# Short attentions with their scores in two halves and other products between; third one with three groups combined ahead and blocks 1, 2, 2, 3, 3

## What is computed

```
h = tok(x)                                   # patches @ W + b + positions
h = LN(h + attn0(h))   # 12 heads of 16, scores minus 0.2 x 3x3 neighbour sum, softmax
h = LN(h + ffn0(h))    # causal attention, then 8 experts, top 2, capacity
h = LN(h + attn1(h))   # scale per head, diagonal masked, projection with bias
h = LN(h + ffn1(h))    # 4 layers: attention (12 heads of 64, relative bias), FFN, experts in 2 of them
```

## Time and profile before

| | us |
|---|---|
| three runs | 1920.93, 1916.85, 1915.08 |
| median | 1916.85 |
| the profiled execution, its own time | 1923.19 |
| its span in the profile | 1921.4 |
| mean granted TensorE clock of the span | 0.842 |
| PE busy | 1628.4 (85%) |
| DVE busy | 1066.7 (56%) |
| ACT busy | 803.4 (42%) |
| POOL busy | 514.1 (27%) |

### The profile page before, as it was taken

How to read it: one execution, slowest core, us unless ns; L and a number is a source line. 1 busy time by engine, 2 the same in 40 slices (tenths; PEclk the granted TensorE clock), 3 DMA queues, 4 the chain that set the end, 5 groups by cost and what they waited for, 6 DMA issues and landing times.

```text
span 1921.4 us, 33734 instructions
## 1 busy us (share of the span) xinstructions
PE 1628.4 (85%) x11941; PEld 1507.5 (78%) x11941; DVE 1066.7 (56%) x2975; ACT 803.4 (42%) x1914; POOL 514.1 (27%) x1259
## 2 busy tenths in 40 slices
PE   5889996984988998999988999698989998899970
PEld 4878775984777997989877999588888997789970
DVE  3575555333645676557764443367755678434337
ACT  1444431433555554355433454245534544255420
POOL 2245334005422112612331000453235132300030
PEclk6766755995657999999889999779989989899985
DMA  4120101440097000100004666200010000256620
GB/s 143 32 78 10 42 20 49 149 159 26 23 284 223 1 2 27 53 1 6 15 28 141 205 217 199 71 15 1 1 63 18 1 15 16 63 180 214 210 88 26
DMA packets 78394, 149.76 MB, mean 78 GB/s; under 512 B 6340, under 2 KB 57843, under 8 KB 78230
## 3 DMA queue, kind: packets, MB, share of 16 engines
q1 hardware_dynamic: 71894, 135.35, 21.7%
q0 software_dynamic: 6336, 12.26, 2.2%
HBM read 106.59 MB, written 41.05 MB: 77 GB/s over the span
## 4 chain that ended last, share of the span: by engine, by line
PE 53%; issue 17%; DVE 16%; DMA 5%; ACT 5%; POOL 2%; SPq 1%; another core or an unknown queue 0%; DVEq 0%; POOLq 0%; ACTq 0%
PE ps_proj L1058 10%; PE ps_proj L1181 6%; PE ps_score L1252 6%; PE ps_proj L1072 5%; PE ps_o L1153 4%; PE ps_pt L1023 4%; PE ps_proj L1235 4%; PE ps_score L1109 4%; DMA w_in<-w_all_dram 4%; PE ps_o L1143 3%; PE ps_score L1120 2%; ACT w_hi L1400 2%; PE ps_proj L1039 1%; DVE prob L1581 1%; DVE negmax L1583 1%
## 5 line engine op out<-in xcount | busy, mean ns | idle before, releaser
L1252 PE MATMUL ps_score<-w,hid 128*112 128x192 f32 (+2 forms) x1680 | 305.5, 334 | 9.5 <-DVE x L1892 9.5
L1252 PEld LDWEIGHTS ps_score<-w,hid 128*112 128x112 f32 (+2 forms) x1680 | 277.8, 180 | 11.8 <-DVE x L1892 11.1
L1376 ACT ACTIVATE hid<-ps_proj 128x224 f32<-128x224 f32 (+2 forms) x360 | 133.8, 382 | 266.8 <-PE ps_proj L1235 253.9
L1481 POOL TENSOR_SCALAR tmp<-rs,var 111x1 f32<-111x1 f32 x110 | 40.9, 372 | 626.8 <-DVE rs L1552 626.3
L1439 POOL DMA_INDIRECT tin<-rows_out,idx x66 | 68.3, 1035 | 482.9 <-issue 377.1
L1023 PE MATMUL ps_pt<-const,prob 111*111 111x111 f32 x660 | 128.3, 313 | 36.7 <-ACT probt L1364 24.9
L1181 PE MATMUL ps_proj<-wo,ot 128*111 128x192 f32 (+1 forms) x616 | 143.5, 384 | 3.9 <-ACT ot L1342 3.7
L1023 PEld LDWEIGHTS ps_pt<-const,prob 111*111 111x111 f32 x660 | 96.2, 205 | 57.1 <-issue 25.9
L1364 ACT ACTIVATE probt<-ps_pt 111x333 f32<-111x333 f32 x176 | 78.9, 448 | 130.2 <-PE ps_pt L1023 128.8
L1181 PEld LDWEIGHTS ps_proj<-wo,ot 128*111 128x111 f32 (+1 forms) x616 | 115.6, 209 | 15.6 <-issue 12.8
L1153 PEld LDWEIGHTS ps_o<-v,probt 111*111 111x111 f32 x1056 | 127.3, 193 | 0.4
(11 more groups left out here) (255 smaller groups left out, 4212.9 us busy)
## 6 DMA issues: line engine op xcount, KB each, us to landing
w_in<-w_all_dram SPq DMA_DIRECT2D x65, 768.0 KB, 4.2
w<-w_all_dram SPq DMA_DIRECT2D x50, 576.0 KB, 5.1
rows_in<-zero SPq DMA_DIRECT2D x1, 12320.0 KB, 47.0
rows_out<-zero SPq DMA_DIRECT2D x1, 9240.0 KB, 79.2
tin<-rows_in SPq DMA_DIRECT2D x36, 224.0 KB
rows_out<-tout SPq DMA_DIRECT2D x36, 168.0 KB
patch<-patches_dram SPq DMA_DIRECT2D x11, 333.0 KB, 3.0
wo<-wo_all_dram SPq DMA_DIRECT2D x6, 576.0 KB, 3.9
```

The lines of the kernel that those rows point to most:

```text
L1252: last = pe.matmul(bank[0:n, 0:C], hid[:, i % 2, m, at:at + n], w2[:, slot, m, :], start=(m == 0), stop=(m == FC - 1))
L1376: act.activation(hid[:, i % 2, m, 0:n], bank[:, 0:n], ACT.Relu if b.tile is None else ACT.Gelu).then_inc(taken, 1)
```

## The change

- The scores of a short attention are made in two halves, S (mask and first chunk of heads) and a new step SB (second chunk, `short_scores`). V(n) moves from the slot behind PV of the step before to between S(n) and SB(n); in the first attention TOK(n+7) goes there too, ahead of V(n). The softmax shift on VectorE moves from S to SB.
- A new helper `dense` issues, behind the first half, two products of 128 x 128 weights with 512 columns of the query and key weights into ps_pt, whose result nobody reads. It does so for every group but the first of the second and third attention, and for groups 4 to 10 of the first; it waits for the copy of the transposed probabilities of group n-2.
- Third attention: the blocks of groups are 1, 2, 2, 3, 3 instead of 1, 2, 2, 2, 2, 2. The lead combines groups 0, 1 and 2 before the first QK and score products; gathers 2 to 5 take new places; the turns of groups 1 and 2 go ahead of S(0). From then on `DIAG_COMB` says which groups are combined in which step, and their norm and turn come one step later. The QK products of block 1 move ahead of E(0).

The diff:

```diff
--- before.py
+++ after.py
@@ -51,7 +51,8 @@
 
 
 NEIGH, CAUSAL, DIAG, T5 = 0, 1, 2, 3
-DIAG_BLOCKS = [(0, 1), (1, 2), (3, 2), (5, 2), (7, 2), (9, 2)]
+DIAG_BLOCKS = [(0, 1), (1, 2), (3, 2), (5, 3), (8, 3)]
+DIAG_COMB = {0: [3], 1: [4], 2: [5], 3: [6, 7], 4: [8], 5: [9], 6: [10]}
 NATT = 3 + LAYERS
 
 
@@ -163,7 +164,7 @@
 def first_block(a):
 
     s = ATTS[a]
-    return [("QK", 0, j) for j in range(s.qk)] + [("V", 0, j) for j in range(s.vparts)]
+    return [("QK", 0, j) for j in range(s.qk)] + [("V", 0, j) for j in range(s.vparts) if not s.short]
 
 
 def neigh_lead():
@@ -171,7 +172,7 @@
     return [("TOK", 0), ("TOK", 1), ("W1", LOAD0[("att", NEIGH)]), ("TOK", 2), ("NX", 0), ("A", 0), ("TOK", 3), ("NX", 1),
             ("A", 1), ("TOK", 4), ("NX", 2), ("A", 2), ("QK", 0, 0), ("QK", 0, 1), ("TOK", 5), ("BD", 0, 0),
             ("QK", 0, 2), ("QK", 0, 3), ("QS", 0, 0, 0), ("QS", 0, 0, 1), ("BD", 0, 1), ("NX", 3), ("TOK", 6),
-            ("V", 0, 0), ("QS", 0, 1, 0), ("QS", 0, 1, 1), ("NX", 4), ("NX", 5)]
+            ("QS", 0, 1, 0), ("QS", 0, 1, 1), ("NX", 4), ("NX", 5)]
 
 
 COMB_AT = {0: ((3, 0), (4, 1)), 1: ((5, 1), (6, 4)), 2: ((7, 4),), 3: ((8, 1),), 4: ((9, 1),), 5: ((10, 1),)}
@@ -197,18 +198,15 @@
         i = n - s.blocks[b][0]
         last = i == s.blocks[b][1] - 1
         if a == DIAG:
+            for c in DIAG_COMB.get(n - 1, ()):
+                slots[0].append(("prev", ("NC", c)))
+                slots[1].append(("A", c))
             if n == 0:
-                slots[0] += combine(1) + combine(2) + [x for g in (1, 2) for x in (("prev", ("NC", g)), ("A", g))]
-            else:
-                slots[0] += [("prev", ("NC", n + 2))] * (n + 2 < G)
-            if n + 3 < G:
-                slots[0 if n else 2] += combine(n + 3)
-            if n and n + 2 < G:
-                slots[1 if last else 2].append(("A", n + 2))
-        if n + 1 < G:
-            slots[2].append(("V", n + 1, 0))
-        if a == DIAG and last and b + 1 < len(s.blocks):
-            slots[2] += [("QK", b + 1, j) for j in (0, 2, 1, 3)]
+                slots[0].append(("prev", ("GAT", 6)))
+            for c in DIAG_COMB.get(n, ()):
+                slots[0] += combine(c)
+            if last and b + 1 < len(s.blocks):
+                slots[0 if n == 0 else 2] += [("QK", b + 1, j) for j in (0, 2, 1, 3)]
         elif a != DIAG and b + 1 < len(s.blocks):
             g0, size = s.blocks[b + 1]
             places = [(0, 0), (0, 1), (0, 2)] if a == NEIGH else [(0, 1), (0, 2), (1, 0)]
@@ -226,8 +224,6 @@
                 for k in range(3):
                     slots[k] += [("QS", b + 1, *x) for x in NEIGH_QS.get((i, k), ())]
     if a == NEIGH:
-        if n + 7 < G:
-            slots[1].append(("TOK", n + 7))
         if n + 6 < G:
             slots[2].append(("NX", n + 6))
         if n == 3:
@@ -269,11 +265,16 @@
 
 def short_order(a, last_stage, follower):
 
-    out = neigh_lead() if a == NEIGH else first_block(a) if last_stage[0] == "ffn" else []
+    out = neigh_lead() if a == NEIGH else []
+    if a == DIAG:
+        out += first_block(a) + [("A", 1), ("prev", ("NC", 2)), ("A", 2)]
     for n in range(G + 2):
         slots = short_fill(a, n, last_stage, follower)
         if n < G:
             out.append(("S", n, 0))
+            if a == NEIGH and n + 7 < G:
+                out.append(("TOK", n + 7))
+            out += [("V", n, 0), ("SB", n)]
         out += slots[0]
         if a == NEIGH and n >= 3:
             out.append(("XA", n - 3))
@@ -415,7 +416,8 @@
             if m % 2 and k:
                 out.append(("D", k - 1, m // 2))
     out += [("D", E - 1, p) for p in range(parts)]
-    out += [("GAT", 0), ("GAT", 1), ("COMB", 0), ("GAT", 2), ("GAT", 3), ("NC", 0), ("GAT", 4), ("next", ("A", 0))]
+    out += [("GAT", 0), ("GAT", 1), ("GAT", 2), ("COMB", 0), ("COMB", 1), ("NC", 0), ("next", ("A", 0)), ("COMB", 2),
+            ("GAT", 3), ("GAT", 4), ("GAT", 5), ("NC", 1)]
     return out
 
 
@@ -1023,6 +1025,36 @@
                     last = pe.transpose(ps_pt[0:TG, i * TG:(i + 1) * TG], src, ident)
                 last.then_inc(pt_full, 1)
 
+            def dense(a, g):
+
+                n = unit(a, g - 1, 0) if g else 0
+                if not n or a == NEIGH and g + 7 < G:
+                    return
+                pe.wait_ge(pt_taken, n)
+                full = w1_hi[:, LOAD0[("att", a)] % W_RING, :, :].rearrange("p c n -> p (c n)")
+                for _ in range(2):
+                    pe.matmul(ps_pt[:, 0:512], full[:, 0:128], full[:, 0:512], start=True, stop=True,
+                              skip_group_check=True)
+
+            def short_scores(st, g, j):
+                a = st[1]
+                b = ATTS[a].block_of[g]
+                g0 = ATTS[a].blocks[b][0]
+                banks = [ps_score[:, e, :] for e in range(2)]
+                parts = [(short_q(b % 2), short_k(b % 2))]
+                if a == NEIGH:
+                    parts.append((qband[:, b % 2, :, :, :, :], neigh_kb(b % 2)))
+                for i in range(IPG):
+                    t0 = (g - g0) * TP + i * NTOK
+                    for part, (q_t, k_t) in enumerate(parts):
+                        for e, bank in enumerate(banks):
+                            at, col = 64 * e, (j * IPG + i) * NTOK
+                            ins = pe.matmul(bank[0:TG, col:col + NTOK], q_t[at:at + 64, j, g - g0, i, :],
+                                            k_t[at:at + 64, j, t0:t0 + NTOK], start=(a == NEIGH and part == 0),
+                                            stop=(part == len(parts) - 1), skip_group_check=True)
+                            if (j, i, part) == (1, IPG - 1, len(parts) - 1):
+                                ins.then_inc(score_full, 1)
+
             def att_step(st, step):
                 a = st[1]
                 s = ATTS[a]
@@ -1077,6 +1109,8 @@
                         last = pe.matmul(bank[0:TG, 0:C], const[0:1, K_ONES:K_ONES + TG], early[0:1, Y_VB:Y_VB + C],
                                          start=False, stop=True)
                     last.then_inc(proj_full, 1)
+                elif kind == "SB":
+                    short_scores(st, g, 1)
                 elif kind == "S":
                     p = step[2]
                     banks = [score_bank((*key, e)) for e in range(2)]
@@ -1091,28 +1125,13 @@
                             pe.wait_ge(band_done, 2 * (b + 1))
                     t0 = (g - s.blocks[b][0]) * TP
                     if s.short:
-                        if SCORE[(*key, 0)] % 2:
-                            banks.reverse()
                         for bank in banks:
                             if a != NEIGH:
                                 pe.matmul(bank[0:TG, 0:2 * TG], identb[:],
                                           maskb[:, a, 0:2, :].rearrange("p h k -> p (h k)"),
                                           start=True, stop=False, skip_group_check=True)
-                        parts = [(short_q(b % 2), short_k(b % 2))]
-                        if a == NEIGH:
-                            parts.append((qband[:, b % 2, :, :, :, :], neigh_kb(b % 2)))
-                        for j in range(2):
-                            for i in range(IPG):
-                                for part, (q_t, k_t) in enumerate(parts):
-                                    for e, bank in enumerate(banks):
-                                        at, col = 64 * e, (j * IPG + i) * NTOK
-                                        ins = pe.matmul(bank[0:TG, col:col + NTOK],
-                                                        q_t[at:at + 64, j, g - s.blocks[b][0], i, :],
-                                                        k_t[at:at + 64, j, t0 + i * NTOK:t0 + (i + 1) * NTOK],
-                                                        start=(a == NEIGH and part == 0),
-                                                        stop=(part == len(parts) - 1), skip_group_check=True)
-                                        if (j, i, part) == (1, IPG - 1, len(parts) - 1):
-                                            ins.then_inc(score_full, 1)
+                        short_scores(st, g, 0)
+                        dense(a, g)
                         return
                     for i in range(3):
                         for e, bank in enumerate(banks):
@@ -1746,11 +1765,11 @@
                 elif kind == "S":
                     if step[1:] == (0, 0) and st[1] == CAUSAL:
                         link(dve.memset(v64[:, :, :, T5_D:T5_D + 1], 1.0))
-                    if ATTS[st[1]].short:
-                        short_shift(st, step[1])
-                    else:
+                    if not ATTS[st[1]].short:
                         for e in range(2):
                             softmax_shift(st, step[1], 2 * step[2] + e, (*key, e))
+                elif kind == "SB":
+                    short_shift(st, step[1])
                 elif kind == "PV":
```

## The result

The changed kernel takes 1942.22 us (median of 14 runs, 1919.47 to 1958.14) against 1913.09 (14 runs, 1899.4 to 1922.53); the ratio is 1.0112, with a 95% interval of 1.0082 to 1.0142. It is slower by 1.1%, some 21 us, where 30 us less were forecast and the range ended at 1915. The ratio leaves out three slow runs of the changed kernel (1949.36, 1953.54 and 1958.14 us); the median of its other eleven is 1933.67, and that is the number to hold against 1913.09. The profiled execution took 1933.23 us (span 1931.4, mean clock 0.854, before 0.842).

The account below looks back on a forecast made before the run. TensorE, busy 85% of the span, was taken to bound the kernel, with 260 us of the short attentions at half clock. The terms -40 + 18 - 10 - 1 + 3 = -30 gave 1887 us from a 1916.85 median; range 1845 to 1915.

Parts of the forecast that it names:

- Falls and rises (-40): Three short attentions: wide products between score halves stop some falls of TensorE's clock to half level; -40 us together.
- my own factor 0.43: TensorE in the short attentions: gain of 0.43 us taken for each us turned from half to full clock.
- The signs that I had named: Short attentions: mean clock about 0.8, fewer than 11 of 33 score runs at half level, median score instruction below 378 ns.
- the very fall that I had counted as gone: First attention: the clock fall behind group 8 goes, so groups 9 and 10 run at full level; two steps, -10 us.
- the second rival: Short attentions: clock level stays, PV and QK lose the value product beside them; slower by 13.5 us, 1930 us; chance 0.12.
- its worse case of 1941: Short attentions: as the second rival, with 26 us more at half level; 1941 us.
- The dense products (+18): Between score halves: 27 pairs of 512 columns on TensorE's path, 0.47 or 0.97 us a pair; +18 us.
- The embedding (+3): First attention, four groups: the moved embedding no longer hides ScalarE's copy before PV, a 0.74 us wait each; +3 us.
- The lead (-10): Third attention's start: waits for the rows of groups 1 and 2 go under block 0's QK products; -10 us.
- the blocks (-1): Third attention: 100 instead of 120 QK instructions, one block fewer and one 0.99 us wait saved; -1 us.
- Rival (3): Third attention: the lead gives nothing, GpSimd's gathers move the wait from group 1 to group 3; 1897 us; chance 0.12.

Follow-up runs that it names:

- no_dense: The changed kernel without the two dense products per group, scores still in halves with value and embedding products moved; ratio 1.0055 to the kernel before, 1923.42 us.
- third_only: The kernel before with only the third attention's new order (lead, combine steps, blocks 1,2,2,3,3); ratio 0.9935 to the kernel before, 1901.71 us.
- old_third: The changed kernel with the third attention's lead, combine steps and blocks put back as before; ratio 1.0134 to the kernel before, 1935.74 us.
- first_both: third_only plus, in the first attention, dense products and value product between the score halves, embedding in its old place; ratio 0.9981 to the kernel before, 1906.91 us.
- again: The changed kernel measured once more with no edit; ratio 1.0128 to the kernel before, 1933.72 us.
- third_dense: third_only plus dense products between the score halves in all three attentions, value and embedding in their old places; ratio 1.0031 to the kernel before, 1920.41 us.
- third_causal2: third_only plus dense products alone between the score halves of the second attention, value product in its old place; ratio 1.0009 to the kernel before, 1920.56 us.
- first_dense: third_only plus seven dense pairs between the score halves of the first attention, value and embedding in their old places; ratio 0.9940 to the kernel before, 1895.71 us.
- third_grouped: third_only with the second attention's four QK products of a block together behind one PV; ratio 0.9954 to the kernel before, 1907.79 us.

## Why the prediction was wrong

**Falls and rises (-40): the step that failed.** I let wide products between the halves stop the falls, and turned 93 us (40 / 0.43). Twice the missing clock times the stretch gives the half-level time, as before. First, second and third attention: before 73.1, 69.4 and 86.4 us, together 228.9; after 80.5, 47.7 and 83.5, together 211.7; the change once more 80.6, 47.7 and 104.9, together 233.2. So between 17 us turned and 4 lost. Only the second attention gained, 22 us, worth 9 by my own factor 0.43, and its ten pairs took 7 of them (seven behind a half run at full level at 0.56, three at 1.02): 105.2 to 103.7 us. By single profiles the pairs did turn something: no_dense has 249.6 us at half level, 16 to 38 more than the two profiles with them, worth 7 to 16 us by the same factor, and that is less than the 21.6 us of work that they add. The signs that I had named say the same. The mean clock was to be about 0.8 and is 0.67, 0.77 and 0.62. Of 66 half runs of scores 32 are at half level and two partly, where a third at most was forecast. The median score instruction is 298 ns in the form without the band and 378 in that with it:

```profile
L1052 PE MATMUL ps_score<-qk x792: 254/298/400, 50.4 to 582.2; 64*111 64x37 f32 x198
L1052 PE MATMUL ps_score<-qk,qband x264: 262/378/379, 50.6 to 181.1; 64*111 64x37 f32 x132
```

How a fall comes nevertheless shows in the timeline of the changed kernel's TensorE, group 8 of the first attention, the very fall that I had counted as gone and priced at 10 us:

```profile
155.26 0.73 PE L1036 MATMUL ps_pt<-w_hi 128*128 128x512 f32 x2
...
158.20 0.64 PE L1025 MATMUL ps_pt<-const,prob 111*111 111x111 f32 x4
159.64 2.19 PE L1162 MATMUL ps_o<-vimg,probt 111*37 111x51 f32 x24 [0.80 <-ACT probt L1381]
...
164.14 1.22 PE L1036 MATMUL ps_pt<-w_hi 128*128 128x512 f32 x2
165.16 0.36 PE L1104 MATMUL ps_proj<-w_hi,xa_hi 128*111 128x192 f32 x1
```

The pair and the value product run at full level, the second half of the scores too, and then PV is at half level, 2.19 us, behind a wait of 0.80. The wide work is where I wanted it, and the fall comes at the same product as before: in the earlier trace rows PV of this group has 2.26 us behind a wait of 0.74. Transposes and PV still stand in one piece with the second half. I had seen in the earlier trace rows that the level falls behind a score run and took the run for its cause, when PV and the transposes are small products as well. Both falls also have a wait just ahead of them, so these lines do not tell the small products from the gap.

**The value product, which I moved at no cost.** This is the second rival, and it is the one that came: PV and QK lose the wide product beside them. Alone its move measured +0.33, +0.26 and +0.49% in the three attentions, and +0.41% in the first beside the dense products: four times the same sign, together some 21 us by the first three. Each is about as large as its interval, and three of them lean on the same base; what is clear of noise is the move of value and embedding together, 23 us (no_dense against third_only). That lost clock is the cause is shown for the second attention only (105 us in eight profiles, 109.8 and 110.0 in the two with the move, all of it busy time). In the third, 110.6 and 112.4 us lie just above the scatter of the unchanged stretch, and in the first 0.69 stays and 107.6 us lies inside it. There it remains argued. The rival gave 1930 us on the base of 1917, +0.7%; measured is +1.1%, between it and its worse case of 1941, +1.3%.

**The dense products (+18).** The price is nearly right: forecast 0.47 and 0.97 us a pair, measured 0.56 and 1.02, and 11 to 18 us in the whole. The wider products that I had missed in the trace before change nothing: 128 x 384, a start every 0.17 to 0.18 us at full level, gives the same 0.24 us for 512 columns. Wrong was that clock would pay for it.

**The embedding (+3).** The place was right and the term was mis-sized: +7.5 us, of which 6.1 are idle. I asked how long ScalarE's copy would be waited for and not what else on TensorE's path came late under this cover; it was VectorE's rows, 4.9 us more of waits in the pair that differs in nothing else (6.2 in the changed kernel). I had said that VectorE's work ahead of the shift costs nothing, and looked there at its readers in the next step only.

**The lead (-10) and the blocks (-1).** Right in sum: third_only is 12 us faster, and of that the lead has 9.1; the 1 us of the blocks is too small to be seen here. In the changed kernel the turn of group 1 waits for nothing and that of group 2 for 1.60 us, where the earlier trace rows had 7.29 and 4.34, and the second score run stands 31.8 us behind the first gather, 42.1 before: 10.3 sooner.

```profile
454.00 0.42 PE L997 MATMUL ps_turn<-const,x 111*128 111x111 f32 x1
...
456.59 0.42 PE L997 MATMUL ps_turn<-const,x 111*128 111x111 f32 x1 [1.60 <-DVE xb L1741]
```

Rival (3) is out. In the full change the whole time does not resolve the gain (old_third), only the stretch does.

**The rule of the Trainium skill.** The Trainium skill, "TensorE: Matmul & The Clock Gate", section "Why this matters for your kernels", wants no idle gaps, and I set it aside because a step without idle stood at half level. That row stands. As a warning the rule would still have served: the change made gaps, 6.6 us of idle in the first attention. But that the gaps held the clock down is not shown. With dense products and the value product between, the first attention stands at 0.72 where the embedding has its old place (first_both, 8.0 us idle), and at 0.67, 0.67 and 0.73 where it is moved (the change, again, old_third, 14.7 to 15.6 us idle); the last of these:

```profile
64.00:177.70 113.70, 98.99 (x932) 87.97 (x932) 65.24 (x169) 47.76 (x116) 38.19 (x113) 0.73 0.13 39
```

**The sum by what was measured**: third order -12, value +21, embedding +7.5, dense products +14 give about +30; measured are +21 and +24. Without the dense products about +16 is the sum and +10.5 the measurement (the moves taken together are +23 and not +28.5); the intervals of the parts, each some 5 to 7 us to either side, cover the difference.

**What stays open.** The dense products are not additive. One attention at a time, value between in the first and second and third, they measured +0.13, -0.33 and -0.12%, together -0.3%, but +0.6 to +0.7% in the full change and +0.96% in third_dense, where +0.74% come from the second alone (third_causal2). The second attention with dense products has two outcomes, and no run here tests what chooses between them.

## What to carry to other kernels

Ask of each product that is moved what it covered for every engine, and look for the latest of them over all groups, the first ones above all, where one-time work stands. Where levels of the clock are to be turned, look at all small products in a row and not at the longest group of them, count what the moved wide product leaves bare in its old place, and try the filler work alone before it is paid for. Take the parts of a change one at a time: here one part of four was a gain, and the others hid it. And before a stretch of one profile is read, look at the same stretch in kernels that leave it alone: one stage repeated to 0.5 us here, its neighbours only to 6 and 8.

## What the hardware showed that I had not expected

The same code in the same place takes different times, mostly by the clock. The part behind the third attention, 8207 products, took 1299.7 (old_third, clock 0.93) to 1322.8 us (the change, 0.91) over the kernels here; TensorE's busy time in it ran from 1114.6 to 1138.0 us, its idle time from 171 to 189. The eleven runs of the changed kernel that its ratio rests on spread from 1919.47 to 1946.93. So a change upstream that shifts the start of a stage can cost or give 10 us where nothing was touched, and a gain of 5 us in one stretch (first_dense, third_grouped) may not arrive in the whole.
